# Folded decay and value projections in the second block's recurrent layer of a two-block decoder

## The reference, cut to what matters

```python
def _L1_attn_ref(x, omega, Win, Wl, bl, Wv, bv, Wout):
    xz = jnp.einsum('btd,ed->bte', x, Win)
    xi, z = jnp.split(xz, 2, axis=-1)
    log_lam = -C * jax.nn.softplus(omega) * jax.nn.sigmoid(jnp.einsum('bti,ji->btj', xi, Wl) + bl)
    lam = jnp.exp(log_lam)
    v = jnp.einsum('bti,ji->btj', xi, Wv) + bv
    h0 = xi[:, 0]
    def step(h_prev, inp):
        x_t, v_t, lam_t = inp
        vh = jnp.sum(v_t * h_prev, axis=-1, keepdims=True)
        vv = jnp.sum(v_t * v_t, axis=-1, keepdims=True)
        Qh = h_prev - 2.0 * v_t * (vh / vv)
        h = lam_t * Qh + (1.0 - lam_t) * x_t
        return (h, h)
    ...
    return jnp.einsum('bti,di->btd', jax.nn.silu(z) * h, Wout)
```

## Time and profile before

| | |
|---|---|
| median of 3 runs | 930.36 us (929.99 to 931.58) |
| the profiled execution, its own time | 930.63 us |
| its span, first to last instruction | 928.9 us |
| outside the span | 1.73 us |
| mean granted TensorE clock | 0.973 |
| busy: PE, DVE, ACT, POOL | 87%, 82%, 56%, 53% |

### The profile page before, as it was taken

One profiled execution on the slowest core, in us unless ns is written; L12 is line 12 of the kernel. 1 busy time (PEld: TensorE's weight loads), 2 busy tenths in 40 slices (PEclk: granted clock), 3 DMA queues, 4 the chain that ended last, 5 costly groups with the idle time before them and its releaser, 6 DMA issues.

```text
span 928.9 us, 14813 instructions
## 1 busy us (share of the span) xinstructions
PE 808.0 (87%) x5151; PEld 585.1 (63%) x5151; DVE 758.1 (82%) x1379; ACT 518.3 (56%) x956; POOL 496.7 (53%) x498
## 2 busy tenths in 40 slices
PE   8977777777798999999999879999999898999881
PEld 6463232323266788887866556787766677899771
DVE  7499999999988489999847986776999979767663
ACT  5867666666638535555365232316666683078771
POOL 6659999999952021222238833456444400177773
PEclk9979999999999899999999999999999999999996
DMA  7000000000000031223000000000000040186654
GB/s 209 0 1 0 0 1 0 1 0 1 1 1 0 18 111 63 89 99 108 1 1 1 1 1 1 0 2 1 2 3 23 25 114 24 36 152 172 153 132 158
DMA packets 36740, 39.68 MB, mean 43 GB/s; under 512 B 5131, under 2 KB 28697, under 8 KB 35898
## 3 DMA queue, kind: packets, MB, share of 16 engines
q1 hardware_dynamic: 34170, 33.62, 11.9%
q0 software_dynamic: 2496, 5.12, 3.6%
HBM read 30.86 MB, written 7.86 MB: 42 GB/s over the span
## 4 chain that ended last, share of the span: by engine, by line
PE 38%; DVE 19%; POOL 6%; issue 5%; ACT 5%; DMA 2%; POOLq 0%; DVEq 0%; ACTq 0%
PE ps L1785 11%; PE ps L1981 3%; POOL y_rows L655 3%; PE ps L1778 3%; PE ps L2135 2%; PE ps L2055 2%; PE ps L2190 2%; DVE small L1554 2%; PE ps L2325 2%; POOL G L650 2%; DVE R L1515 1%; DMA G<-xn_rows,token 1%; PE ps L1858 1%; DVE G L1557 1%; DVE ps L1520 1%
## 5 line engine op out<-in xcount | busy, mean ns | idle before, releaser
L1785 PE MATMUL ps<-xhl,whl 128*128 128x512 f32 x576 | 144.4, 400 | 3.4 <-ACT G L865 1.5
L1785 PEld LDWEIGHTS ps<-xhl,whl 128*128 128x128 f32 x576 | 108.2, 191 | 28.4 <-issue 3.0
L480 POOL TENSOR_TENSOR R<-G,R 128x1024 f32<-128x1024 f32 x43 | 100.6, 2354 | 7.3 <-ACT R L726 3.8
L1224 DVE TENSOR_TENSOR_SCAN R<-ps,R 128x1024 f32<-128x1024 f32 x43 | 97.6, 2279 | 7.7 <-POOL R L489 5.5
L785 ACT ACTIVATE ps<-G,negAb,negA 128x508 f32<-128x508 f32 x128 | 95.0, 779 | 0.5 <-DVE R L1224 0.5
L1837 PE MATMUL ps<-bc,sel 96*128 96x512 bf16 x128 | 46.3, 389 | 46.2 <-ACT LN L733 23.0
L1858 PE MATMUL ps<-R,ident 128*128 128x512 f32 x172 | 82.0, 599 | 0.0
L726 ACT COPY R<-ps 128x512 f32<-128x512 f32 x64 | 37.4, 585 | 68.5 <-PE ps L1837 68.5
L865 ACT ACTIVATE G<-ps 128x512 f32<-128x512 f32 x72 | 42.8, 599 | 57.2 <-PE ps L1785 56.3
L1837 PEld LDWEIGHTS ps<-bc,sel 96*128 96x128 bf16 x128 | 12.5, 98 | 97.4 <-ACT LN L733 36.0
L650 POOL DMA_INDIRECT G<-xn_rows,token x39 | 39.2, 1005 | 58.9 <-DVE per_tile L1717 45.6
(11 more groups left out here) (375 smaller groups left out, 2144.1 us busy)
## 6 DMA issues: line engine op xcount, KB each, us to landing
R<-in_exp_wi_dram SPq DMA_DIRECT2D x39, 256.0 KB
G<-cw_by_expert SPq DMA_DIRECT2D x6, 1024.0 KB, 4.7
ew<-in_w_dram SPq DMA_DIRECT2D x24, 128.0 KB, 2.2
y_rows<-zeros SPq DMA_DIRECT2D x1, 2048.0 KB, 9.0
xn_rows<-LN SPq DMA_DIRECT2D x8, 256.0 KB
G<-in_exp_wo_dram SPq DMA_DIRECT2D x8, 256.0 KB, 4.5
G<-y_rows SPq DMA_DIRECT2D x4, 512.0 KB, 5.4
X<-in_x_dram SPq DMA_DIRECT2D x4, 256.0 KB
```

The lines of the kernel that those rows point to most:

```text
L480: gp.tensor_tensor(halves(dBu[i % 3]), duT[:, :, gcols(i // NS)], Bsb[:, i % 4:i % 4 + 1, :].broadcast_to([P, HI, GT]), ALU.mult).then_inc ...
L1224: v.tensor_tensor_scan(hst[i % 3], bank(2 * j, 2).rearrange("p h n -> p (h n)"), dBu[i % 3], 0.0, ALU.mult, ALU.add).then_inc(S["scanned"], 1)
L1785: ins = mm(mix(out) if n == N_WIN1 else out, whl[:, wslot(n), i, m * P:(m + 1) * P], rhs, start=k == 0, stop=k == 2)
```

## The change

It has four parts.

**Folded weights.** `xi @ Wl` is `x @ (Win_xi Wl)`, and likewise for `Wv`. The product of the two weights is made once, in the expert loop: at step 11 PE transposes the two `xi` tiles of `Win`, ACT copies them at step 12, PE makes the product at step 13 (four float32 multiplies of 256 columns), ACT and DVE split it into two float32r parts (`lvhl`) at steps 14 and 15. Values and decays are then three multiplies for each tile, straight from `xhl`. They no longer read `xi`.

**New order.** PE begins with the last transposes and values and decays of group 0, then `xz(0)`. `xz(1)` to `xz(3)` come around group 1, and `chunk_dots(0)` before the values of group 2. Twenty-four filler multiplies (`unread(0, 24)`) stand before the last spread. ACT no longer copies `xz(0)`: DVE does. ACT copies the three others in one run behind the decays of group 1, and `e_copy(1)` and `e_copy(2)` come behind the decays of group 3.

**Storage.** The products of odd groups move to a buffer of their own (`kp1`), so DVE no longer waits for all of `xz`; it waits for the two `xi` tiles of its group. POOL zeroes `cp` group by group, a quarter each time.

**Table.** The Exp and Tanh table of ACT is loaded before the third layer norm's scaling, not before the first Exp of group 0.

```diff
@@ expert loop, ACT
+                if i == LV_AT + 1:
+                    wait(act, "wt1_mm", 1)
+                    sc.copy(Win1T, bank(7)[:, 0, 0:HI * P].rearrange("p (k n) -> p k n", k=HI)).then_inc(S["wt1_ev"], 1)
+                if i == LV_AT + 3:
+                    wait(act, "lv_mm", 1)
+                    sc.copy(lvhl[:, 0], bank(6)[:, 0, :]).then_inc(S["lv_hi"], 1)
...
+            sc.preload_act_table_set("exp_and_others")
             for g in range(NG):
                 normalize(3, g)
@@ ACT, the stage
-            xz_copy(0)
             copy_xnT(3, NG - 1)
...
+            for g in range(2):
+                v_copy(g)
+                v_square(g)
+                decays(g)
+                if g:
+                    xz_copy(g)
+            xz_copy(2)
+            xz_copy(3)
+            carry_last(0)
+            e_copy(0)
+            for g in range(2, NG):
+                v_copy(g)
+                v_square(g)
+                decays(g)
+            for g in range(1, NG - 1):
+                carry_last(g)
+                e_copy(g)
@@ expert loop, DVE
+                if i == LV_AT + 4:
+                    wait(dve, "lv_hi", 1)
+                    v.tensor_tensor(lvhl[:, 1], bank(6)[:, 0, :], lvhl[:, 0].bitcast(F32), ALU.subtract).then_inc(S["lv_lo"], 1)
@@ DVE, the stage
-                if g == 1:
-                    dve.wait_ge(S["xz_mm"], 4 * NG)
...
+            for m in range(4):
+                dve.wait_ge(S["xz_mm"], m + 1)
+                v.tensor_copy(row((xi if m < HI else z1)[:, m % HI], 0), mix(bank(4 + m)[:, 0, :])).then_inc(S["xz_ev"], 1)
...
+                dve.wait_ge(S["xz_ev"], 4 * g + HI)
                 v.scalar_tensor_tensor(pos(nb, g), lam_g, 1.0, pos(xi, g), ALU.subtract, ALU.mult).then_inc(S["nb_done"], 1)
@@ POOL
-                if g == 1:
-                    pool.wait_ge(S["xz_ev"], 4 * NG)
-                    gp.memset(cp[:, 0:GT], 0.0)
-                elif g >= 2:
+                if g >= 2:
                     pool.wait_ge(S["dots_mm"], 2 * g - 2)
...
+                pool.wait_ge(S["xz_ev"], 4 * NG if g == 1 else 4 * (g + 1))
+                gp.memset(row(cp, g)[:, 0], 0.0)
@@ expert loop, PE
+                if i == LV_AT:
+                    pe.wait_ge(S["w_lru"], 16 * 6)
+                    for k in range(HI):
+                        ins = nc.tensor.transpose(bank(7)[:, 0, k * P:(k + 1) * P], w["Win1"][:, k, :], ident[:])
+                    ins.then_inc(S["wt1_mm"], 1)
+                if i == LV_AT + 2:
+                    wait(pe, "wt1_ev", 1)
+                    for j, name in enumerate(("Wv", "Wl")):
+                        for k in range(HI):
+                            ins = mm(bank(6)[:, 0, j * DI:(j + 1) * DI], Win1T[:, k, :], w[name][:, k, :], start=k == 0, stop=k == HI - 1)
+                    ins.then_inc(S["lv_mm"], 1)
@@ PE, the stage
-                    for k in range(HI):
-                        ins = mm(mix(bank(banks[m])[:, 0, :]), wt[:, k, m * P:(m + 1) * P], row(xi[:, k], g),
-                                 start=k == 0, stop=k == HI - 1)
+                    elif banks[m]:
+                        pe.wait_ge(S["ln_lo"], 2 * NG + banks[m] + 1)
+                    cols = slice((first + m) * P, (first + m + 1) * P)
+                    for k, (i, j) in enumerate(PARTS):
+                        ins = mm(mix(bank(banks[m])[:, 0, :]), lvhl[:, i, cols], row(xhl[:, j], g), start=k == 0, stop=k == 2)
...
+            transpose_xn(3, NG - 1)
+            lam_and_v(0)
             xz(0)
-            transpose_xn(3, NG - 1)
-            for g in range(NG):
...
+            v_dot_v(0)
+            spread_reciprocal(0)
+            lam_and_v(1)
+            xz(1)
+            v_dot_v(1)
+            xz(2)
+            spread_reciprocal(1)
+            xz(3)
+            chunk_dots(0)
+            lam_and_v(2)
+            v_dot_v(2)
+            spread_reciprocal(2)
+            lam_and_v(3)
+            chunk_dots(1)
+            v_dot_v(3)
+            pe.wait_ge(S["v2_ev"], HI * NG)
+            pe.wait_ge(S["l_ev"], HI * NG)
+            unread(0, 24)
+            spread_reciprocal(3)
+            chunk_dots(2)
             chunk_dots(NG - 1)
```

More of the change, by code:

```diff
@@ L44 @@
 FIRST_ROUND = (10, 18, 26)
+LV_AT = 11
 POOL_HC = (1, 4, 7, 10, 13)
@@ L89, in decoder_program @@
             log_la = moe_sb("log_la", [P, 1])
+            per_tile = moe_sb("per_tile", [P, 6, NT])
+            with nc.sbuf_tensor("kp1", [P, HI * 6 * KG], F32) as kp1:
+                pass
             choice = moe_sb("choice", [P, 2, B, E])
@@ L121, in decoder_program @@
         rvv = sb("rvv", [P, NG, C4])
+        with nc.sbuf_tensor("lvhl", [P, 2, 2 * DI], F32R) as lvhl:
+            pass
         w = {}
@@ L157, in decoder_program @@
         wo_now = R[:, 3, :, :].rearrange("p s (w n) -> p (s w) n", w=2)
+        Win1T = LN[:, 1, 0:HI * P].rearrange("p (k n) -> p k n", k=HI)
         S = {}
@@ L301, in decoder_program @@
         kp = [buf.rearrange("p (h j k) -> p h j k", h=HI, k=KG)
-              for buf in (ew0[:].rearrange("p s w n -> p (s w n)"), seq[:, 0:HI * 6 * KG])]
+              for buf in (ew0[:].rearrange("p s w n -> p (s w n)"), kp1[:])]
         dot_bank = lambda g: 0 if g == NG - 1 else 4
@@ L912, in e_copy, with v_copy @@
                 sc.copy(row(cp, g)[:, 1:C4], e_psum(g).rearrange("p (i k) -> p i k", k=KG)).then_inc(S["e_ev"], 1)
-            xz_copy(0)
             copy_xnT(3, NG - 1)
-            for g in range(NG):
+            def v_copy(g):
                 for m in range(HI):
@@ L920, in _, with v_square @@
                         .then_inc(S["v2_ev"], 1)
+            def v_square(g):
                 act.wait_ge(S["v2_ev"], HI * (g + 1))
@@ L924, in _, with decays @@
                 sc.activation(sq[:, g % 2], pos(vv, g), ACT.Square).then_inc(S["sq_done"], 1)
+            def decays(g):
                 for m in range(HI):
@@ L932, in _ @@
                         .then_inc(S["lam_done"], 1)
-                if g == 0:
-                    xz_copy(1)
-                    xz_copy(2)
-                if g == 1:
[L937 to L940, removed]
+            for g in range(2):
[15 more added lines that the diff above has]
+                e_copy(g)
             carry_last(NG - 1)
@@ L2047, in xz, with lam_or_v @@
                     up(bank(4 + m)[:, 0, :], N_WIN1, m, g).then_inc(S["xz_mm"], 1)
-            def lam_or_v(g, wt, banks, done, freed):
+            def lam_or_v(g, first, banks, done, freed):
                 for m in range(HI):
@@ L2053, in lam_or_v, with lam_and_v @@
                         pe.wait_ge(S[freed[m][0]], freed[m][1])
-                    for k in range(HI):
-                        ins = mm(mix(bank(banks[m])[:, 0, :]), wt[:, k, m * P:(m + 1) * P], row(xi[:, k], g),
-                                 start=k == 0, stop=k == HI - 1)
+                    elif banks[m]:
[3 more added lines that the diff above has]
+                        ins = mm(mix(bank(banks[m])[:, 0, :]), lvhl[:, i, cols], row(xhl[:, j], g), start=k == 0, stop=k == 2)
                     ins.then_inc(S[done], 1)
+            def lam_and_v(g):
+                pe.wait_ge(S["ln_lo"], 2 * NG + g + 1)
+                lam_or_v(g, 0, (0, 1), "v2_mm", (("l_ev", HI * g), ("v2_ev", HI * g)))
+                lam_or_v(g, HI, (2, 0), "l_mm", (("l_ev", HI * g - 1), ("v2_ev", HI * g + 1)))
             def v_dot_v(g):
@@ L2096, in chunk_dots @@
                 ins.then_inc(S["dots_mm"], 1)
+            wait(pe, "lv_lo", 1)
+            pe.wait_ge(S["res0"], (E + 1) * NG)
+            transpose_xn(3, NG - 1)
+            lam_and_v(0)
             xz(0)
-            transpose_xn(3, NG - 1)
-            for g in range(NG):
-                pe.wait_ge(S["xz_ev"], 4 * g + HI)
-                if g == 0:
-                    pe.wait_ge(S["ln_lo"], 2 * NG + 3)
-                lam_or_v(g, w["Wv"], (0, 1), "v2_mm", (("l_ev", HI * g), ("v2_ev", HI * g)))
-                lam_or_v(g, w["Wl"], (2, 0), "l_mm", (("l_ev", HI * g - 1), ("v2_ev", HI * g + 1)))
-                v_dot_v(g)
-                spread_reciprocal(g)
-                if g == 0:
-                    xz(1)
-                    xz(2)
-                if g == 1:
-                    xz(3)
-                if g:
-                    chunk_dots(g - 1)
+            v_dot_v(0)
[18 more added lines that the diff above has]
+            chunk_dots(2)
             chunk_dots(NG - 1)
```

6 lines of the change are left out of this document (1 added, 5 removed).

## The result

| | before | after |
|---|---|---|
| median of 13 runs each, same sitting | 930.17 us | 923.39 us |
| lowest to highest | 927.39 to 933.67 | 917.64 to 928.05 |
| ratio, 95% interval | | 0.9924 (0.9903 to 0.9945) |
| profiled execution, its own time / span | 930.63 / 928.9 | 918.88 / 916.8 |
| busy: PE, DVE, ACT, POOL | 87, 82, 56, 53% | 87, 83, 56, 55% |

The change makes the kernel 7.1 us faster (5.1 to 9.0 by the interval). The forecast was 8.85 us faster, or 921.5 us.

The account below looks back on a forecast made before the run. PE was taken to bound the experts and the start of the changed stage, then DVE from first reciprocal to last solve. Terms +2.0 - 4.65 - 6.7 + 0.5 = -8.85 us gave 921.5 us, range 918.8 to 925.8.

Parts of the forecast that it names:

- term 3: First reciprocal to last solve: all of DVE's 6.8 us of waits go, 0.1 left as margin; -6.7 us.
- term 4: Same stretch: DVE without gaps has POOL beside it more, so its wide operations slow; +0.5 us, bounds 0 to 1.8.
- Term 1: Expert stage: folding adds two transposes and four multiplies to PE, all on the path; +2.0 us, bounds 1.7 to 2.7.
- Term 2: Start of the changed stage: DVE's first reciprocal comes at 472.25 instead of 476.90; -4.65 us, table load put at 0.
- The two bold places: Tightest hand-overs in the stage: e_copy(0) behind twelve copies, 1.3 us of slack; fillers before spread 3, 0.5 us.
- rival A: PE slow after idle, or late copies, make DVE wait again: 1.5 to 4 us, say 924; chance 0.22 with Rival D.
- The signs: Right if experts' PE adds 2 us, first reciprocal comes 4.65 sooner, DVE then waits under 1, last solve 66 later.
- signs of being wrong: L1466 waits for L2144 or L927, L1483 for L2116, clock under 1.00 before last spread, or L1443 to L1450 longer.
- Rival C: PE idles more in the changed stage, its clock falls to half: 15 us lost, 936 us; chance 0.05.
- Rival D: Expert loop: inserted work lets DVE's backlog stall PE, 2 us at most, 923.5; chance 0.22 together with rival A.

Follow-up runs that it names:

- e6: Changed kernel with nine filler multiplies on PE before the spread of group 2: 948.60 us, ratio 0.9937 to the kernel before.
- both repairs: Changed kernel with POOL's decay products ahead of its nb wait in group 0 and nine fillers before spread 2: 927.01 us, ratio 0.9950.
- e2: Kernel before with folded weights used and the changed storage, but old order, ACT copies and table load: 954.47 us, ratio 0.9987.

## Why the prediction was right, and where it was not

- **The whole.** Forecast 921.5 us, measured 923.39. The errors of the terms add up and don't cancel (term 3 by 1.5 us, term 4 by 0.4, the others by 0.2 or less), so it is not by luck that the time lies in the range.
- **Term 1, the folding, +2.0: right.** 1.95 in the chain of the changed kernel and of the fold by itself, 2.0 and 2.1 by the length of the stage.
- **Term 2, the first reciprocal, -4.65: right to 0.2.** -4.49. The squared norms still end last (1.04 us of wait), and the decays are there before them, as worked out. That the table load could be put at nothing is shown by its removal.
- **Term 3, the waits, -6.7: the direction right, the size wrong by 1.5.** 1.56 us are left, so -5.2. The step that failed is the line "POOL does 54.87 us for four groups, 13.7 each; it starts at 473.7 and is never later than DVE's need". The total was taken over from a stretch in which POOL idled between the groups. I priced the contention for DVE (term 4) and put it at nothing for POOL, without a reason. Without its idle time POOL stood beside 35.6 instead of 30.1 us of the operations of DVE that slow it, the same sixty products and the zeroing took 58.48 us, groups 0 and 1 18.2 and 14.6 instead of 15.4 and 12.7, and the last solve came to wait for them. Term by term: 54.87 us, 2.4 us between its 64 instructions, which I had left out, and 3.6 of slowing (0.3 of it for zeroing by groups) are 60.9, from 1.6 us after the reciprocal: 62.5. By my own figures POOL would have been done at 1.45 + 54.9 = 56.3 and the last solve wanted it at 65.8 - 5.5 (the solve itself) = 60.3, 4 us of room for the 6 that came on top. I had asked only for `e_in` and group 2, not for the last products of group 3. (A slip beside it: `xz(2)` ends at 483.6 by its own durations, not at 483.2; nothing hangs on it.)
- **The two bold places** held. `e_copy(0)` is done at 490.5 for a solve at 492.06, 1.5 us of slack (forecast 1.3), and the fillers end 0.3 us before the last reciprocal (forecast 0.5). So rival A did not come by its places. Its mechanism did, where the rival had its evidence and at a smaller size: PE idles 2.46 us before spread 2 (forecast 2.3), the spread takes 1.94 instead of 1.16 us, and DVE waits 0.55, 0.28 or 0.17 us for it in three executions of the changed kernel. Taking it away gave nothing by itself (`e6`). Of the 1.9 us by which the time came nearer to rival A's 924, 1.0 is POOL's wait, which neither account had.
- **Term 4, contention, +0.5: 0.9.** DVE's 84 instructions took 0.91 us more, within the bounds. With both repairs the stretch is 66.9 us, of which 0.47 is a wait: 65.7 plus 0.7.
- **The signs.** "DVE waits under 1 us", with the last solve ending "some 66 us later", did not come: 1.56 and 68.15 us. Of the signs of being wrong, none of the waits came, the clock before the last spread was 1.00 (507 to 515 us) though 0.65 around spread 2 (497 to 500), and L1443 to L1450 were 0.5 us longer in sum. The wait that did come, L1466 for L589, was not on the list.
- **Rival C** (the clock falls through the stage) did not come: 0.92 was granted in the third stretch (0.95 before), and even where it was 0.83 (`e2`) the stretch was 1.7 us shorter than before. **Rival D** did not come either; the experts lost 1.95 to 2.1 us and no more.

## What to carry to other kernels

When waits of the busiest engine are removed, add up the next busiest one over the same stretch again, to the last thing it must deliver, with durations as they are beside a busy neighbour. Where a delay on one engine is swallowed and one on the other is paid in full, they end together, and a repair has to shorten both. A gain of 1 us is read from stretches between the kernel's own events; spans and even medians of a dozen runs carry several us of clock. Fillers counted for one gap come out too few when PE gets sooner: 24 of them left 0.5, then 2.0 us.

## What the runs showed of the hardware

- A 128x256 product on POOL took 0.70 to 0.75 us beside DVE's operations with an input in PSUM or beside an idle DVE, and up to 1.7 us beside DVE's operations with both inputs in SBUF. Over the third stretch POOL's sixty products and zeroing went from 54.87 to 58.48 us by that, and DVE's 84 instructions from 63.74 to 64.65.
- After some 2.45 us of idle the same eight multiplies of the spread took 1.16, 1.57, 1.66, 1.94, 2.01, 2.06 and 2.07 us in seven executions.
- The granted clock varies between executions in stretches that no edit touched: 0.89 or 1.00 at 300 to 330 us, 0.50 or 1.00 for 11.6 us of attention. The 13 runs of the changed kernel span 10.4 us; the lowest, 917.64, had a mean clock of 0.975, the highest, 928.05, 0.967.
- The kernel before took 955.5 us in one sitting and 930.9 in another on a chip of the same number. In the slower one the changed kernel was granted 0.93 from 750 to 900 us and its DMAs moved 97 GB/s (first stretch below), in the other 0.98 and 117 GB/s (second):

```profile
750.00:900.00 150.00, 125.86 (x982) 114.26 (x980) 93.01 (x257) 74.56 (x148) 60.75 (x60) 0.93 0.44 97
```

```profile
750.00:900.00 150.00, 135.92 (x1098) 126.06 (x1096) 109.03 (x291) 91.45 (x185) 77.96 (x76) 0.98 0.51 117
```

  What made the sittings differ stays open.
